# Attention output products of a head moved into the next head's steps, in a graph network kernel on one core

## What is computed

```python
for i in range(NUM_BLOCKS):                      # 4
    y = _cond_layer_norm(x, cond, s1_w[i], s1_b[i], b1_w[i], b1_b[i])
    q = (y @ wq + bq).reshape(N, H, Dh) * Dh ** (-0.5)      # H = 4, Dh = 128
    k = (y @ wk + bk).reshape(N, H, Dh)
    v = (y @ wv + bv).reshape(N, H, Dh)
    scores = jnp.einsum('ehd,ehd->eh', q[src], k[dst])
    smax = jax.ops.segment_max(scores, src, num_segments=N)
    ex = jnp.exp(scores - smax[src])
    denom = jax.ops.segment_sum(ex, src, num_segments=N)
    out = jax.ops.segment_sum((ex / denom[src])[:, :, None] * v[dst], src, num_segments=N)
    x = x + out.reshape(N, D) @ wo + bo
    y = _cond_layer_norm(x, cond, s2_w[i], s2_b[i], b2_w[i], b2_b[i])
    x = x + jax.nn.relu(y @ m_w1[i] + m_b1[i]) @ m_w2[i] + m_b2[i]
```

## Time and profile before

| | us |
|---|---|
| median of three runs | 3648.99 (3648.54 to 3649.54) |
| the profiled execution | 3659.81 |
| its span, first to last instruction | 3658.1 |
| TensorE busy | 3096.1 (85%) |
| VectorE busy | 1908.1 (52%) |
| GpSimd busy | 833.4 (23%) |
| ScalarE busy | 749.6 (20%) |
| mean granted clock of TensorE | 0.915 of 2.4 GHz |

### The profile page before, as it was taken

The page is one execution under the profiler, slowest core; times in us unless marked ns, Lnnn a source line. Parts: engine busy times, 40 slices in busy tenths (PEclk is TensorE's granted clock), DMA queues, the critical chain, the costliest instruction groups (busy, mean ns, idle before and its releaser), DMA issues.

```text
span 3658.1 us, 35312 instructions
## 1 busy us (share of the span) xinstructions
PE 3096.1 (85%) x12190; PEld 1990.9 (54%) x12190; DVE 1908.1 (52%) x3612; ACT 749.6 (20%) x1046; POOL 833.4 (23%) x623
## 2 busy tenths in 40 slices
PE   4877359999889998989998899998387498898999
PEld 0344236667556666556666456675144355565555
DVE  9977225665236664235674246662279788412111
ACT  0142121222212222212222112222020111212221
POOL 5632121334222333123334113342010100000100
PEclk9988669999999999999999999999779599799899
DMA  4011210000000000000000100000335445201000
GB/s 137 4 32 32 81 46 12 1 24 1 30 27 12 1 24 18 23 28 1 24 1 18 38 12 1 24 1 18 94 110 149 136 130 146 72 12 58 12 1 28
DMA packets 83715, 147.69 MB, mean 40 GB/s; under 512 B 22047, under 2 KB 22438, under 8 KB 83528
## 3 DMA queue, kind: packets, MB, share of 16 engines
q1 hardware_dynamic: 61604, 121.16, 10.8%
q0 software_dynamic: 20624, 20.99, 2.0%
q10 hardware_dynamic: 1300, 3.13, 0.3%
HBM read 126.95 MB, written 30.37 MB: 43 GB/s over the span
## 4 chain that ended last, share of the span: by engine, by line
PE 52%; issue 17%; DVE 13%; POOL 5%; DVEq 4%; DMA 4%; ACT 3%; POOLq 1%; SPq 1%; ACTq 0%
PE ps L1287 11%; PE ps L1296 8%; PE ps L1484 7%; PE ps L1381 6%; PE ps L1438 4%; DVEq L928 4%; POOL pacc L589 3%; DMA typed_t<-run,rowi 3%; DVE big L926 2%; PE ps L1354 2%; PE ps L1476 2%; PE ps L1369 2%; PE ps L1372 2%; PE ps L1370 2%; PE ps L1371 2%
## 5 line engine op out<-in xcount | busy, mean ns | idle before, releaser
L589 POOL TENSOR_TENSOR pacc<-pacc,prob 125x628 f32<-125x628 f32 (+1 forms) x288 | 404.2, 1403 | 332.2 <-DVE prob L877 332.2
L1381 PE MATMUL ps<-prob,big 125*128 125x314 f32 x1280 | 404.7, 438 | 21.1 <-DVE prob L877 15.6
L1296 PE MATMUL ps<-yT,w 128*128 128x416 f32 (+1 forms) x1152 | 410.3, 516 | 6.9 <-ACT yT L1094 6.9
L1484 PE MATMUL ps<-pieces,counts_r 125*125 125x512 f32 x1400 | 359.3, 412 | 28.9 <-DVE x L953 15.5
L1132 ACT ACTIVATE prob<-ps 125x628 f32<-125x628 f32 x320 | 222.3, 695 | 747.1 <-PE ps L1372 738.2
L877 DVE SCALAR_TENSOR_TENSOR prob<-prob,ct 125x628 f32<-125x628 f32 x320 | 311.3, 973 | 100.3 <-ACT prob L1132 100.3
L1484 PEld LDWEIGHTS ps<-pieces,counts_r 125*125 125x125 f32 x1400 | 262.5, 189 | 121.4 <-DVE x L953 22.2
L1296 PEld LDWEIGHTS ps<-yT,w 128*128 128x128 f32 x1152 | 218.3, 190 | 190.3 <-issue 189.1
L1287 PE MATMUL ps<-w,yT 128*125 128x512 f32 x640 | 290.9, 601 | 12.6 <-DVE pieces L940 11.8
L1287 PE MATMUL ps<-w,big 128*125 128x512 f32 x640 | 282.7, 601 | 3.7 <-issue 3.0
L1369 PE MATMUL ps<-qk_hi 128*125 128x314 f32 x640 | 273.3, 427 | 8.5 <-ACT prob L1132 6.3
(11 more groups left out here) (198 smaller groups left out, 4366.2 us busy)
## 6 DMA issues: line engine op xcount, KB each, us to landing
basis<-in_basis SPq DMA_DIRECT2D x240, 256.0 KB, 2.6
w<-in_m_w SPq DMA_DIRECT2D x8, 1024.0 KB, 6.6
typed_t<-zero_row SPq DMA_DIRECT2D x20, 305.2 KB
ct<-typed_t POOLq DMA_DIRECT2D x2, 3051.8 KB, 39.4
w<-in_wv SPq DMA_DIRECT2D x5, 1024.0 KB, 5.7
w<-in_wq SPq DMA_DIRECT2D x5, 1024.0 KB, 5.5
w<-in_wk SPq DMA_DIRECT2D x5, 1024.0 KB, 5.3
oT<-in_cw SPq DMA_DIRECT2D x9, 512.0 KB, 6.3
```

The lines of the kernel that those rows point to most:

```text
L589: nc.gpsimd.tensor_tensor(pacc[:, c0:c0 + nn], pacc[:, c0:c0 + nn], prob[:, n % 3, p0:p0 + nn], ALU.add).then_inc(psum_done, 1)
L1296: last = mm(lin_ps(job, 128, nn), weight[:, k, m * 128:(m + 1) * 128], lhs[:, k, c0:c0 + nn], start=(k == 0), stop=(k == KD - 1))
L1381: last = mm(o_halves[:, b, :], vrow[:, t, h * DH:(h + 1) * DH], prob[:, n % 3, b * QUARTER:(b + 1) * QUARTER], start=(t == 0), stop=(t == ...
L1484: last = mm(lin_ps(job, P, D), counts_r[:, slot, k, :], pieces[:, piece, k, :], start=(self_ is None and k == 0 and piece == 0), stop=(k = ...
```

## The change

The output product of head h no longer stands between the heads. For h of 0 to 2 its ten tiles run in steps 0 to 9 of head h+1, one a step, behind the weighted values of the step before (`attended`); VectorE adds tile j-1 behind the masked probabilities of step j (`add_out`). ScalarE's first copy to `oT` in head h+1 waits until all ten tiles have been read. The product of head 3 stays where it was.

The six projection jobs of head h+2 are split in three: the first goes ahead of the last weighted values of head h, the next three behind them, then come the row of maxima and the denominators, and the last two follow the denominators. At the start of the block the row of maxima of head 0 goes between the fourth and the fifth projection of head 1, and VectorE negates the maxima ahead of that head's `qk_lo` parts. The waits for the row and for the last projections move from behind the row to the head's start (`row_written`) and to its first `max_scores` (`projected`).

```diff
+PARTS = {None: range(6), 0: range(0, 1), 1: range(1, 4), 2: range(4, 6)}
@@ plan_block
-    project(1)
+    project(1, 0)
+    project(1, 1)
     max_row(0)
+    project(1, 2)
     for h in range(HEADS):
-        project(h + 2)
+        if h:
+            g["out"][h - 1] = [w.take() for _ in range(T)]
+        project(h + 2, 0)
+        project(h + 2, 1)
         max_row(h + 1)
         g["den"][h] = w.take()
-        g["out"][h] = [w.take() for _ in range(T)]
+        project(h + 2, 2)
+    g["out"][HEADS - 1] = [w.take() for _ in range(T)]
@@ VectorE
+                negate_max(0)
                 low_parts(1)
-                negate_max(0)
+
+                def add_out(h, t):
+                    job = g["out"][h][t]
+                    dve.wait_ge(lin_full, job.full)
+                    V.scalar_tensor_tensor(out=x[:, t, :], in0=lin_ps(job, P, D), scalar=rden[:, t:t + 1],
+                                           in1=x[:, t, :], op0=ALU.mult, op1=ALU.add).then_inc(lin_empty[job.slot], 1)
+
                 for h in range(HEADS):
+                    if h == 1:
+                        dve.wait_ge(xbias_done, at(i, 2, 1))
                     for j in range(2 * T):
...
+                        if h and 1 <= j <= T:
+                            add_out(h - 1, j - 1)
                     if h + 1 < HEADS:
                         negate_max(h + 1)
                     if h + 2 < HEADS:
-                        low_parts(h + 2)
+                        low_parts(h + 2, 0)
+                        low_parts(h + 2, 1)
...
+                    if h + 2 < HEADS:
+                        low_parts(h + 2, 2)
@@ ScalarE
+                    if h and half == 0:
+                        act.wait_ge(lin_full, g["out"][h - 1][-1].full)
...
+                    if h + 2 < HEADS:
+                        high_parts(h + 2, 0)
                     copy_o(h, 1)
                     if h + 2 < HEADS:
-                        high_parts(h + 2)
+                        high_parts(h + 2, 1)
                     if h + 1 < HEADS:
                         max_row(h + 1)
+                    if h + 2 < HEADS:
+                        high_parts(h + 2, 2)
@@ TensorE
                 for h in range(HEADS):
+                    row_written(h)
                     for j in range(2 * T):
                         exp_scores(h, j)
                         if h + 1 < HEADS:
+                            if j == 0:
+                                projected(h + 1)
                             max_scores(h + 1, j)
                         if j:
                             weighted_values(h, j - 1)
+                        if h and j < T:
+                            if j == 0:
+                                pe.wait_ge(o_copied, at(i, 2 * HEADS, 2 * h))
+                                if h == 1:
+                                    pe.wait_ge(w_in[0], at(i, 32, 32))
+                            attended(h - 1, j)
+                    if h + 2 < HEADS:
+                        project(h + 2, 0)
                     weighted_values(h, 2 * T - 1)
                     if h + 2 < HEADS:
-                        project(h + 2)
+                        project(h + 2, 1)
                     if h + 1 < HEADS:
                         max_row(h + 1)
-                    if h + 2 < HEADS:
-                        projected(h + 2)
 
                     job = g["den"][h]
...
-                    pe.wait_ge(o_copied, at(i, 2 * HEADS, 2 * h + 2))
-                    for t, job in enumerate(g["out"][h]):
-                        reuse(job)
-                        mm(lin_ps(job, P, D), oT[:, t * P:(t + 1) * P], w[0][:, h, :], start=True, stop=True).then_inc(lin_full, 1)
+                    if h + 2 < HEADS:
+                        project(h + 2, 2)
+                pe.wait_ge(o_copied, at(i, 2 * HEADS, 2 * HEADS))
+                for t in range(T):
+                    attended(HEADS - 1, t)
```

## The result

The changed kernel is faster. The first four timed executions had a median of 3598.06 us (3590.82 to 3607.24) against 3649.26 us; its ratio to the kernel before was 0.9846, with a 95% interval from 0.9801 to 0.9891. Timed again with more executions of both, the ratio was 0.9845 (0.9826 to 0.9865), 3596.99 us against 3657.31: 60 us less by the medians, 57 us by the ratio (49 to 64), which is not the quotient of the two medians. The forecast was 3604 us, 45 us less. Single executions of the kernel before lie between 3641 and 3672 us, of the changed one between 3591 and 3610, so a pair of them tells the gain to some 10 us only. The kernel before had a median of 3649 us at first, 3657 beside the first four experiments and 3654 and 3653 beside the last six, so a few us between medians of different groups say nothing; the two profiles differ by 62 us in their spans (3658.1 and 3596.0).

A forecast was written before the change was run, and what follows sets the result against it. TensorE's work was taken to bound the steps and nearly all of the stretches between heads. Per block 2 x 4.0 + 1.8 + 1.5 = 11.3 us, four times 45: 3649 - 45 = 3604 us, eight-in-ten range 3588 to 3628.

The forecast's parts named there:

- Rival D: Output tiles in the steps: a wait taken as covered puts them back to 1.07 us each, 3629; 0.16 shared with another rival.
- Term 1: Stretches between heads 0 and 1 and heads 1 and 2: 29.45 us instead of a mean of 39.64, 10.2 us less.
- Term 2: Ten early steps of heads 1 and 2, now with output tiles: 32.6 us instead of 26.4, 6.2 us more.
- Term 3: Between heads 2 and 3, 9.4 us less; ten early steps of head 3, 7.6 us more; net 1.8 us less.
- Term 4: Start of a block: 1.0 us less waiting for negated maxima and 0.5 us less from the lower clock, together 1.5 us.
- Rival A': Stretches between heads: the clock falls less; if the low time halves, 23 us, giving 3581; chance 0.13.
- rival B: Early steps: VectorE's addition and GpSimd take turns, a step takes 4.0 us instead of 3.36, kernel 3654; chance 0.05.
- Rival C: Lower clock outlasts the stretch into the next head's early steps, 5 us more in each of twelve, 3664; chance 0.04.

The follow-up runs named there:

- early row: Changed kernel with the row of maxima moved ahead of the second to fourth projection: 3573.79 us, ratio 0.9788; timed again 3573.18 us, 0.9780.

## Why the prediction was right, and where it was off

**The bound and the direction were right.** The steps are TensorE's: an output tile in them costs 3.36 - 2.50 = 0.86 us, the value of the earlier trace rows, and no 1.07; the new waits that the prediction called covered (bank, copy to `oT`) do not appear in the steps. Rival D falls with that. The prediction gave two reasons for the 1.07 us; at full clock the banks' turn alone makes it 0.98, and the rest is the lower clock.

**Term 1 gave 29.45 us for the stretch, it is 28.20.** With 3.4 us at the lower level the stretch lasts 26.95, with 6.8 us 28.6: each microsecond at it costs half of one, as the term had it, and at full clock 25.25 us remain, where the sum gave 25.95. Its pieces were each a little long (weighted values with handover 1.06 and not 1.17, projections 2.70 and not 2.75). The rest is the clock: 6.0 us a stretch at the lower level in this profile and not 7.0. The 7.0 came from three stretches; all eight of the kernel before had 6.4 in the mean.

**Term 2 was too small by 0.6 us.** The steps 3 to 9 behind the first are 3.36 us as forecast. The first three are 2.9, 3.2 and 3.5 us, 9.6 together, where the sum had 9.1. Of the half microsecond 0.1 is the missing set of weighted values, worth 1.06 us and not 1.17, and 0.1 the wait of the first maximum scores, 0.30 us and not 0.2; the rest is not attributed. The waiting did go (0.14 us idle of 33.15). It was larger than the 1.4 us of the prediction, which counted ten sets of weighted values in the old steps, where there are nine as in the new: 26.4 - (25.0 - 1.06) = 2.5 us.

**Term 3 gave 1.8 us net, the profiles show 3.1.** The stretch is 11.0 and not 12.8 us, with 3.4 to 6.8 us at the lower level where 6.6 were charged, and the overlong pieces again. The wait behind the row fell by the 0.3 us that were counted, from 0.51 to 0.19, but the last weighted values wait 1.03 us there instead of 0.71 (block 0), which takes it back. The steps are 0.5 us longer than forecast, since the lower clock lasted 0.4 to 1.7 us into them. At full clock they are as forecast: in the second profile of the changed kernel the one head 3 without a fall takes 29.72 us.

**Term 4 was mis-sized the most.** 1.5 us was forecast for a block's start, and it is 2.6 between the blocks and 0.45 in head 0's steps: 3 us, four times. Over the kernel the terms are short by some 4 us (1 and 2 together), 5 us (3) and 6 us (4), which makes of the forecast's 45 us the 61 of the profiles. Term 2 alone erred to the other side. The wait for the negated maxima went as foreseen. The clock did not fall at any start, where half of one was granted. Put back, the start costs 11 us by the profile and by the ratio, 16 by the medians.

**Rival A' was the way in which it missed.** The lower clock took 78.5 us in the twelve stretches and 20.5 in three of four starts before; after, 68.3 and nothing. Half of the difference is 15 us, and the profiles' gain is 16 us above the forecast; A' was priced at 23 us for half of the low time. The prediction charged the same low time as before because the short work ahead of the fall was "the same and as long". The early row shows how sensitive that is: with the same instructions in another order two of eight stretches had a fall. That the forecast nevertheless came within 7 us of the first median is in part luck: the kernel before ran 8 us slower beside the second measurement, and the gain is 57 to 60 us where 45 was said.

**VectorE and rival B.** The addition took 0.73 us beside GpSimd's, so the step is TensorE's. Of the two readings of the rule in the Trainium skill ("SBUF — State Buffer", section "SBUF: two separate sides") the one in which only tensors count holds: a tensor and a column of scalars in SBUF did not exclude GpSimd, two tensors did. The price that B was given was wrong even for the case in which it applies: 3.51 us and not 4.0. The sum charged VectorE's three instructions 0.80, 0.80 and 0.75 us, where they follow each other every 0.73, two handovers that do not appear, and GpSimd's whole 1.52 us behind the addition, where 1.32 us are left of it.

**Rival C did not come.** The early steps ran at 1.00 and 0.99; the lower clock reached only the first step of head 3, for at most 1.7 us.

## What to carry to other kernels

A product that another engine reads out of two banks in turn belongs between work that does not use those banks: here a tile cost 0.98 us in a row at full clock (1.07 with the lower clock in it) and 0.86 us one a step, and its reader became free of charge. By the estimate above that was a quarter of the gain; the moved work also filled waits in the steps (some 19 us), and the time at the lower clock fell (some 15 us). Short, thin matmuls that stand together (a row of single lines, sums by a column of ones) cost more than their length when the clock falls behind them; the same instructions with dense work between them saved a further 21 to 24 us, four fifths of it by the clock. When an engine beside the bound loses a little each step, look for the price where the steps get shorter, not where the work was added.

## What the runs showed of the hardware

- TensorE counts as busy in the trace during products of one column, and its clock fell all the same: with nine of ten left out the low stretches went from twelve in twelve (eleven in a second execution) to three. With the ten moved behind the next head's first scores, away from the row, it fell in six of twelve places.
- Low stretches between heads came as 3.4, 6.8 or 10.2 us, and two executions of the changed kernel had them at the same places but one, in part with different lengths. The executions of the changed kernel spread over 19 us and those of the kernel before over 31. What stands behind the last exponential took 1176.8 to 1189.3 us in the twelve profiles, with 275 to 299 us of it at the lower clock.
- VectorE's instruction with one tensor in PSUM, one in SBUF and a column of scalars in SBUF (0.73 us) and GpSimd's addition (1.54 us) overlap for 0.58 us without loss; with two tensors in SBUF GpSimd's took 1.97 us and VectorE's next such instruction, of one element, 1.39 instead of 0.15 us.
